# A decoder layer on one core: the exponent bias of each head and two steps of the gate move from VectorE to GpSimd

## The reference, cut to what matters

```python
# 1, own attention: 16 heads of 16, the softmax runs over the heads of one token
scores = einsum('bshd,bstd->bsht', q, k) / 4;  attn = einsum('bsht,bstd->bshd', softmax(scores), v) @ Wo.T
# 2, cross attention: each of 2048 queries against all 2048 keys, 16 heads, q, k, v and the weights quantised
attn = softmax(einsum('bhqd,bhkd->bhqk', q, k))          # q, k rounded to 127 steps of their largest value
attn = round(attn / (max(attn) / 255)) * (max(attn) / 255);  out = (attn @ v) @ Wp + bp
# 3, eight experts, two for each token, and a shared one
scores = sigmoid(xt @ gate.T);  _, sel = top_k(scores + expert_bias, 2)
```

## Time and profile before

| | value |
|---|---|
| median of three runs | 1011.39 us |
| the profiled execution | 1009.28 us, its span from first to last instruction 1007.5 us |
| mean granted TensorE clock | 0.859 of full speed |
| busy share of the span | DVE 90%, POOL 74%, ACT 73%, PE 72%, PEld 40% |
| DMA share of the 16 engines, main queue | 86.7% |

### The profile page before, as it was taken

One profiled execution on the slowest core, in us unless ns is written; L12 is line 12 of the kernel. 1 busy time (PEld: TensorE's weight loads), 2 busy tenths in 40 slices (PEclk: granted clock), 3 DMA queues, 4 the chain that ended last, 5 costly groups with the idle time before them and its releaser, 6 DMA issues.

```text
span 1007.5 us, 21210 instructions
## 1 busy us (share of the span) xinstructions
PE 722.3 (72%) x7072; PEld 398.6 (40%) x7072; DVE 910.5 (90%) x1841; ACT 733.1 (73%) x989; POOL 748.0 (74%) x728
## 2 busy tenths in 40 slices
PE   6965766777677768687777777686868777777674
PEld 4543222344343434343444434343434444343243
DVE  3896967999999999999999999999999999999942
ACT  2633756878877888787777778788878878787842
POOL 6689988979797979797897979797979889710000
PEclk9986786989997989888888979798988889797955
DMA  6011795999899999999998999999999989999971
GB/s 238 1 43 47 131 168 105 173 153 184 169 183 172 157 174 159 167 173 172 166 173 161 180 157 192 170 158 174 169 158 172 175 163 169 158 195 163 192 147 31
DMA packets 574018, 156.01 MB, mean 155 GB/s; under 512 B 567251, under 2 KB 571862, under 8 KB 573526
## 3 DMA queue, kind: packets, MB, share of 16 engines
q1 hardware_dynamic: 573910, 154.67, 86.7%
HBM read 9.93 MB, written 2.10 MB: 12 GB/s over the span
## 4 chain that ended last, share of the span: by engine, by line
DVE 45%; issue 24%; PE 19%; ACT 4%; DMA 2%; SPq 2%; POOL 2%; DVEq 0%; POOLq 0%; ACTq 0%
DVE score L1134 30%; PE ps_score L1458 7%; PE ps L1316 6%; DVE gate L1168 3%; ACT prob L824 2%; PE ps_score L1316 2%; SPq L423 2%; DVE exp_bias L1144 2%; DVE early L1184 2%; DMA prob_t<-prob 2%; ACT queries L806 1%; DVE gate L1166 1%; DVE q_parts L1117 1%; PE ps_pv L1488 1%; PE ps L1437 1%
## 5 line engine op out<-in xcount | busy, mean ns | idle before, releaser
L1134 DVE TENSOR_SCALAR_CACHE_REDUCE score<-ps_score,q_neg 128x1024 f32<-128x1024 f32 x512 | 636.2, 1278 | 17.0 <-PE ps_score L1458 15.5
L824 ACT ACTIVATE prob<-score,exp_bias 128x2048 uint16<-128x2048 f32 x256 | 511.1, 1997 | 11.6 <-DVE exp_bias L1144 9.3
L1458 PE MATMUL ps_score<-keys,queries 128*128 128x512 bf16 x1024 | 351.8, 444 | 195.0 <-DVE score L1134 156.3
L1458 PEld LDWEIGHTS ps_score<-keys,queries 128*128 128x128 bf16 x1024 | 75.4, 104 | 370.7 <-DVE score L1134 306.0
L527 POOL TENSOR_TENSOR product<-hs_exp,v_tok 128x1024 f32<-128x1024 f32 x64 | 148.5, 2342 | 18.0 <-ACT hs_exp L789 17.9
L534 POOL TENSOR_TENSOR product<-product 128x512 f32<-128x512 f32 x128 | 158.9, 1263 | 0.0
L527 POOL TENSOR_TENSOR product<-qk_rot 128x1024 f32<-128x1024 f32 x64 | 149.6, 2350 | 0.3 <-POOL qk_rot L520 0.2
L545 POOL TENSOR_TENSOR product<-product 128x512 f32<-128x512 f32 x64 | 82.4, 1288 | 5.9 <-POOL product L534 5.9
L877 ACT ACTIVATE routed_both<-normed,routed_gate 128x256 bf16<-128x256 f32 x128 | 57.1, 496 | 37.8 <-DVE routed_gate L1179 37.8
L1488 PE MATMUL ps_pv<-prob_t,values 128*32 128x128 f16 x4096 | 73.0, 227 | 11.0 <-DMA prob_t<-prob 10.9
L1488 PEld LDWEIGHTS ps_pv<-prob_t,values 128*32 128x32 f16 x4096 | 62.0, 101 | 40.4 <-issue 40.4
(11 more groups left out here) (124 smaller groups left out, 1125.8 us busy)
## 6 DMA issues: line engine op xcount, KB each, us to landing
prob_t<-prob SPq DMA_TRANSPOSE x256, 4.7
prob_t<-in_w SPq DMA_DIRECT2D x3, 1024.0 KB, 4.8
x_in<-in_x SPq DMA_DIRECT2D x16, 128.0 KB, 3.1
score<-in_cond_t SPq DMA_DIRECT2D x4, 512.0 KB, 6.6
out<-x_out SPq DMA_DIRECT2D x16, 128.0 KB, 2.5
w_qkv<-in_w_qkv SPq DMA_DIRECT2D x1, 768.0 KB, 4.3
early<-in_w_kv SPq DMA_DIRECT2D x1, 512.0 KB
w_s<-in_w_s SPq DMA_DIRECT2D x3, 128.0 KB
```

The costliest lines, as they stand in the source:

```text
L824: act.activation(prob[:, s, :].bitcast(U16), score[:, s, :], ACT.Exp, bias=exp_bias[:, s:s + 1], scale=-1.0, accum_out=prob_sum[:, t.par, ...
L1134: dve.tensor_scalar(score[:, s, HALF * i:HALF * i + HALF], ps_score[:, score_slot(t.count(H, h), i)].rearrange("p b k -> p (b k)"), q_neg[ ...
L1458: mm = pe.matmul(ps_score[:, score_slot(n, i), b, :], queries[:, t.par, h // 2, h % 2, :], keys[:, h // 2, k0:k0 + KEYS], start=True, stop ...
```

## The change

DVE's `bias` goes and POOL gets a `bias` of its own; the first two steps of `choose` go and POOL gets `gate_sums`. POOL's list is written anew around them: the sixteen biases stand between its products, the two first `value_products` of a tile move from the end of a round to the beginning of the next, where all four are now made, and the folds are interleaved. SP's store and load move within the round. Two new functions and POOL's and SP's lists:

```diff
@@ -434,12 +434,12 @@
 
 def body(t):
     for h in range(H):
-        if (t + -2).exists() and h == 13:
+        if (t + -2).exists() and h == 5:
             store(t + -2)
-        if (t + 3).exists() and h == 11:
-            load_x(t + 3)
         if t.exists() and by_dma(h):
             turn(h, t)
+        if (t + 3).exists() and h == 9:
+            load_x(t + 3)
         if (t + -1).exists() and h == 12:
             turn_routed(t + -1)
 
@@ -490,6 +490,29 @@
         pool.sem_inc(settled, 1)
     pool.tensor_tensor(ho_n[:], ho[:], over(hs_inv[:], HD), ALU.mult).then_inc(ho_done, 1)
 
+def bias(h, t):
+    pool.wait_ge(score_kept, t.count(2 * H, 2 * h + 2))
+    pool.sem_inc(settled, 1)
+    if (due := t.due(H, h - RING + 1)) is not None:
+        pool.wait_ge(prob_ready, due)
+        pool.sem_inc(settled, 1)
+    s = h % RING
+    pool.tensor_scalar(exp_bias[:, s:s + 1], low[:, s, 0:1], low[:, s, 1:2], LN255, ALU.min, ALU.add
+        ).then_inc(bias_ready, 1)
+
+def gate_sums(t):
+
+    sig, biased = gate[:, 0, :], gate[:, 1, :]
+    pool.wait_ge(gate_tanhed, t.count(1, 1))
+    pool.sem_inc(settled, 1)
+    if (due := t.due(6)) is not None:
+        pool.wait_ge(gate_chain, due)
+        pool.sem_inc(settled, 1)
+    pool.tensor_scalar(sig, gate_tanh[:], 0.5, 0.5, ALU.mult, ALU.add).then_inc(gate_chain, 1)
+    pool.wait_ge(gate_chain, t.count(6, 1))
+    pool.sem_inc(settled, 1)
+    pool.tensor_tensor(biased, sig, b_expert[:], ALU.add).then_inc(gate_chain, 1)
+
 def spread_sums(t):
 
     pool.wait_ge(sum_inverted, t.count(1, 1))
@@ -592,56 +615,90 @@
     if a.exists() and not t.starts():
         ln_scale(0, a)
     if n.exists():
+        value_products(0, n)
+        value_products(1, n)
+        fold_one(4, n)
+    if t.exists():
+        bias(0, t)
+    if n.exists():
         value_products(2, n)
+    if t.exists():
+        bias(1, t)
+    if n.exists():
+        fold_one(5, n)
+    if m.exists():
+        spread_sums(m)
+    if t.exists():
+        bias(2, t)
+    if n.exists():
         value_products(3, n)
         fold_one(6, n)
         fold_one(7, n)
+    if t.exists():
+        bias(3, t)
+    if n.exists():
+        fold_8(2, n)
         fold_8(3, n)
-    if m.exists():
-        spread_sums(m)
+        fold_4(2, n)
+    if t.exists():
+        bias(4, t)
     if n.exists():
         fold_4(3, n)
+        fold_2(2, n)
         fold_2(3, n)
-    if a.exists():
-        rope(a)
+    if t.exists():
+        bias(5, t)
+        bias(6, t)
     if n.exists():
         norm_ho(n)
     if a.exists():
-        score_products(0, a)
+        rope(a)
     if m.exists():
         ln_scale(2, m)
+    if t.exists():
+        bias(7, t)
+    if a.exists():
+        score_products(0, a)
+    if t.exists():
+        bias(8, t)
+        bias(9, t)
     if a.exists():
         score_products(1, a)
-        score_products(2, a)
-        fold_one(0, a)
-        fold_one(1, a)
-        score_products(3, a)
     if n.exists():
         ln_scale(1, n)
+    if t.exists():
+        bias(10, t)
+    if m.exists():
+        gate_sums(m)
     if a.exists():
-        fold_8(0, a)
-        fold_4(0, a)
+        score_products(2, a)
+    if t.exists():
+        bias(11, t)
+    if a.exists():
+        fold_one(0, a)
+    if t.exists():
+        bias(12, t)
+    if a.exists():
+        score_products(3, a)
+        fold_one(1, a)
+    if t.exists():
+        bias(13, t)
+    if a.exists():
         fold_one(2, a)
         fold_one(3, a)
+        fold_8(0, a)
+        fold_8(1, a)
+        fold_4(0, a)
+    if t.exists():
+        bias(14, t)
+    if a.exists():
+        fold_4(1, a)
         fold_2(0, a)
-        fold_8(1, a)
-        fold_4(1, a)
         fold_2(1, a)
+    if t.exists():
+        bias(15, t)
+    if a.exists():
         shift_scores(a)
-        value_products(0, a)
-        value_products(1, a)
-        fold_one(4, a)
-        fold_one(5, a)
-        fold_8(2, a)
-        fold_4(2, a)
-        fold_2(2, a)
-
-def fold_all(i, t):
-    fold_one(2 * i, t)
-    fold_one(2 * i + 1, t)
-    fold_8(i, t)
-    fold_4(i, t)
-    fold_2(i, t)
 
 def all_scores(t):
     score_products(0, t)
@@ -688,10 +745,6 @@
 all_scores(second)
 shift_scores(second)
 ln_scale(0, Tile(2))
-value_products(0, second)
-value_products(1, second)
-fold_all(2, second)
-
 over_tiles(body)
 
 
@@ -889,63 +942,65 @@
```

In DVE's part:

```diff
@@ -1135,15 +1190,6 @@
                           q_neg[:, t.par, h:h + 1], None, ALU.mult, ALU.min,
                           accum_out=low[:, s, i:i + 1]).then_inc(score_kept, 1)
 
-def bias(h, t):
-
-    dve.wait_ge(score_kept, t.count(2 * H, 2 * h + 2))
-    if (due := t.due(H, h - RING + 1)) is not None:
-        dve.wait_ge(prob_ready, due)
-    s = h % RING
-    dve.tensor_scalar(exp_bias[:, s:s + 1], low[:, s, 0:1], low[:, s, 1:2], LN255, ALU.min, ALU.add
-                      ).then_inc(bias_ready, 1)
-
 def cross_sum(t):
     dve.wait_ge(prob_ready, t.count(H, H))
     if (due := t.due(2)) is not None:
@@ -1162,11 +1208,6 @@
 def choose(t):
 
     sig, biased, marked, best = (gate[:, i, :] for i in range(4))
-    dve.wait_ge(gate_tanhed, t.count(1, 1))
-    dve.tensor_scalar(sig, gate_tanh[:], 0.5, 0.5, ALU.mult, ALU.add).then_inc(gate_chain, 1)
-    dve.wait_ge(gate_chain, t.count(6, 1))
-    dve.scalar_tensor_tensor(out=biased, in0=sig, scalar=1.0, in1=b_expert[:], op0=ALU.mult, op1=ALU.add
-                             ).then_inc(gate_chain, 1)
     dve.wait_ge(gate_chain, t.count(6, 2))
     dve.max(best, biased).then_inc(gate_chain, 1)
     dve.wait_ge(gate_chain, t.count(6, 3))
```

More of the change, by code:

```diff
@@ new lines, in body @@
+                    if m.exists() and h == 8:
+                        ln_combine(2, m)
+                    if t.exists():
+                        keep_scores(h, t)
+                    if m.exists() and h == 11:
+                        choose(m)
+                    if t.starts() and h == 5:
+                        sum_scores(n)
+                    if n.exists() and h == 8 + late:
+                        dve.wait_ge(ho_projected, n.count(1, 1))
+                        ln_gather(1, one_bank(n)[:, 0:D], n)
@@ L1270, in body @@
-                    if m.exists() and h == 5:
+                    if o.exists() and h == 4:
+                        add_out(o)
+                    if m.exists() and h == 7:
+                        dve.wait_ge(xo_projected, m.count(1, 1))
+                        ln_gather(2, bank[6][:, 0:D], m)
+                    if o.exists() and h == 2:
+                        expert_hidden(0, o)
+                    if t.starts() and h == 2:
+                        cast_experts(2)
+                    if a.exists() and h == 15:
+                        largest_score(a)
```

231 lines of the change are left out of this document (106 added, 125 removed).

## The result

The changed kernel takes 1050.82 us (median of four runs, 1046.82 to 1053.82) where the kernel before takes 1011.41 beside it: a ratio of 1.039 [1.0347, 1.0434]. The forecast was 1008, between 985 and 1027.

A forecast was written before the change was run, and what follows sets the result against it. DVE bounded the kernel before, POOL's list after the change. Rounds +7, edges -5.9 - 2.5 - 3.4 + 1.9: -2.9 us from 1009.3 gives 1006.4; the median stands 2.1 higher, 1008.5, rounded to 1008; range 985 to 1027.

The forecast's parts named there:

- DVE as the bound of before, and POOL as the next: Before the change: DVE sets the pace, 1.1 us idle in a 54.62 us round; POOL is next, idle 8.4 us.
- the 95% I named as the sign: Sign that the forecast is right: POOL busy over 95% in a round of 55.2 us.
- The price of a bias (0.38, 0.22 behind another): POOL's sixteen biases: 14 at 0.38 behind a product or fold, 2 at 0.22, so 5.8 us a round.
- The bound of 0.57 on the other side: Upper price of a bias on POOL, from the slowest one-element step (L470): 9.1 us for sixteen.
- the rival that used it: A bias on GpSimd costs double: 0.57 each, a round of 58.5 us, 1051 us in all; chance 0.05.
- The wait of 0.85 us before bias 12: POOL idles before bias 12 for `keep_scores(12)`, as L1179 meets a product and takes 1.65 us: 0.85 us a round.
- `head_exp` at nothing: POOL's wait for this exponential at the round's end costed at nothing, with ACT there some 0.5 us before POOL needs it.
- the slower rival: ACT is late for `head_exp` at the round's end: over 1013.4 us from 0.35 us a round, 1028 at 1.5; chance 0.22.
- The wait of 0.35 us at `shift_scores`: POOL waits for DVE's maximum; bias 15 covers 0.3 of the 0.63 us, so 0.35 remain each round.
- The gate's steps: The gate's two steps on POOL: 0.38, a 0.18 wait for its own result, and 0.22, giving 0.8 us a round.
- The round: POOL's round: 47.4 + 5.8 + 0.8 + 0.35 + 0.85 = 55.2 us, 0.55 more than before; thirteen lose 7 us.
- The edges: Outside the thirteen rounds: first scores of tile 14 -5.9, tile 14 -2.5, tile 15 -3.4, round 0 +1.5, end +0.4 us.

The follow-up runs named there:

- the version with sixteen steps more: Changed kernel with the gate's two steps ahead of the norm's small steps, plus a second, unread one-element instruction behind each of POOL's sixteen biases: 1107.12 us, ratio 1.0956.
- three schedules: Marks in PSUM on the changed kernel with all biases back on DVE (977.37 us), with five biases on POOL (977.73), with the gate early (982.75).

## Why the prediction was wrong

**DVE as the bound of before, and POOL as the next.** Right. DVE's work did fall (49.8 us in the round shown), and POOL sets the round in the changed kernel. But POOL is busy for 88% of that round and not for the 95% I named as the sign: the rest is waits and the gaps around small steps.

**The price of a bias (0.38, 0.22 behind another).** This term failed: 0.50 and 0.37. Fourteen and two make 7.7 us a round instead of 5.8, and 1.9 times 13 is 25 us. The duration was well taken from L474 (0.27; the bias takes 0.29). What was wrong is what follows it: the product behind L474 starts 0.05 us before that step ends, and the one behind a bias 0.08 after its end. The lengthening of the product in front was in the sum. "L474 is the same instruction with other operands" was the sentence that carried the error. The bound of 0.57 on the other side held it, and the rival that used it gave 1051 us and a round of 58.5. That it came out at the number is luck in part: 0.50 instead of 0.57, and the rest from waits. By busy time a bias costs 1.4 times what it does on DVE (0.29 us against 0.21); by what it adds to the engine's list it is 0.50 against 0.13 to 0.24, two to four times.

**The wait of 0.85 us before bias 12.** Right in place, mechanism and size: 1.02 of idle time, 0.92 beyond the gap that any bias has in front of it, and L1220 at 1.71 where 1.65 was used. **`head_exp` at nothing.** This failed too: POOL waits 1.01 us in most rounds, 0.90 on average, for that exponential, since DVE's quantising and so ACT's copy of the queries come late. Both waits go when the collision goes, but this one also shrinks where TensorE's clock is higher. I counted ACT half a microsecond early there and gave the case 0.22; it is the mechanism of the slower rival, whose point of decision, 0.35 us a round, was passed, and half of its cause stood in my own sum.

**The wait of 0.35 us at `shift_scores`.** It stands before bias 15, for the scores of head 15: 0.55 of idle time in most rounds, 0.37 on average beyond the gap of 0.10. The gate's steps cost 0.6, not 0.8.

**The round.** 55.2 + 1.9 (biases) + 0.9 (`head_exp`) + 0.1 (the waits before biases 12 and 15) - 0.2 (gate) = 57.9, against 58.0 measured.

**The edges.** The first scores of tile 14 follow L481 by 0.70 us instead of 6.1: -5.4, forecast -5.9. But tile 14 takes 52.1 us and not 49.4: its POOL still has half a round of products and biases, and in the version with sixteen steps more it takes 55.1, against 51.9 without them. Tile 15 lasts 48.2 us to the last exponential, as long as before and not 3.4 less. DVE's relief isn't on the path there: its last copy ends at 1006.96, 2.6 us before the last exponential starts, and ACT goes through its last three exponentials and the routes between them without a gap. I had applied DVE's saving to two tiles without looking who ends last in them. Round 0 costs 4.5 instead of 1.5, and the end 0.8 instead of 0.4. Sum -4.3 and 4.5 for what I had at -11.4 and 1.5: 10 us.

**The total.** The thirteen rounds lose 44 us instead of 7 and the edges 10 more than forecast; 1006.4 + 37 + 10 = 1053.4 for the profiled execution, which took 1053.8. **The order at nothing.** That was not a term, and should have been one: with both moves undone the new order costs 26 us. In the changed kernel that loss can't be told from POOL's, since another engine sets the pace there, and TensorE's part in it, through the clock, stays open.

## What to carry to other kernels

Price a small instruction by what it does to the distance between the two big ones around it, from a row that has it in just that place. Before work is moved to an idle engine, take apart what is moved: here the move of the two gate steps is worth 59 us in the new order, and the sixteen biases took that and more away. And where a DVE instruction with two SBUF operands can meet a GpSimd product, try one operand from PSUM: with it three schedules that had been up to 21 us apart lay within 5.4. Look at the others too: a DVE step with a single SBUF operand and two constants (L1197) took 2.05 to 2.32 us beside a product in six rounds, and 0.17 otherwise. Last, read the granted clock round by round: a wait that looks like one engine's lateness may come and go with it.

## What the runs showed of the hardware that was not expected

- A one-element step on GpSimd is busy 0.29 us and costs 0.50 between two long instructions, 0.33 to 0.36 behind another small one; one of its two waits less, already met, changed nothing (1029.4 and 1030.2 us).
- A DVE instruction of eight elements takes 0.166 us with one operand from PSUM beside a running GpSimd product, and up to 2.28 us with both in SBUF. With one SBUF operand and two constants it took up to 2.32. The same edit (the gate's steps ahead of the norm's) then changed the time by -21 us in one version and +21 in another, by where that instruction fell.
